# GpSimd writes 13 of the 16 last normed tiles, and the output products use four PSUM banks

## What is computed

```python
def _L1_ffn_ref(x, w_gate, w_up, w_down):
    def act_qdq(x):                       # one scale for the whole tensor
        scale = jnp.maximum(jnp.max(jnp.abs(x)) / 32767., 1e-12)
        return jnp.clip(jnp.round(x / scale), -32768., 32767.) * scale
    x = act_qdq(x)
    up = act_qdq(x @ lpbq_dequant(w_up).T)      # weights: 4 bits, blocks of 32
    gate = act_qdq(x @ lpbq_dequant(w_gate).T)
    sig = fixed_qdq_u16(jax.nn.sigmoid(gate))
    gate = act_qdq(gate * sig)
    o = act_qdq(gate * up)
    return o @ lpbq_dequant(w_down).T
...
x = x + tanh(g_xattn[1]) * _L1_xattn_ref(_layernorm(x), ctx_1024, ctx_1024, ...)
x = x + tanh(g_ffn[1]) * _L1_ffn_ref(_layernorm(x), ...)
```

## Time and profile before

| | |
|---|---|
| median of three runs | 1015.0 us |
| profiled execution | 1014.61 us |
| its span, first to last instruction | 1013.0 us |
| TensorE, VectorE, ScalarE, GpSimd busy | 883.8, 663.7, 477.7, 197.4 us |
| mean granted TensorE clock | 0.921 of 2.4 GHz |

### The profile page before, as it was taken

One profiled execution on the slowest core, in us unless ns is written; L12 is line 12 of the kernel. 1 busy time (PEld: TensorE's weight loads), 2 busy tenths in 40 slices (PEclk: granted clock), 3 DMA queues, 4 the chain that ended last, 5 costly groups with the idle time before them and its releaser, 6 DMA issues.

```text
span 1013.0 us, 13561 instructions
## 1 busy us (share of the span) xinstructions
PE 883.8 (87%) x4064; PEld 437.4 (43%) x4065; DVE 663.7 (66%) x1250; ACT 477.7 (47%) x612; POOL 197.4 (19%) x293
## 2 busy tenths in 40 slices
PE   3989999999974999999987699999999779990088
PEld 2542333333442666666654323333334444430077
DVE  5989888888350222222179788888886763598942
ACT  1323777777730111212132137777777363586650
POOL 3330101111136000000056212100006500124200
PEclk9886999999996999999997769999999999995589
DMA  7593856664243010111168763344310000000001
GB/s 226 151 279 56 206 127 168 162 174 147 88 142 134 32 31 31 31 36 36 49 214 232 176 144 75 85 86 85 80 38 2 1 1 0 1 0 0 0 32 52
DMA packets 71260, 91.45 MB, mean 90 GB/s; under 512 B 25894, under 2 KB 56870, under 8 KB 71206
## 3 DMA queue, kind: packets, MB, share of 16 engines
q1 hardware_dynamic: 62844, 67.38, 26.6%
q0 software_dynamic: 5584, 19.93, 5.9%
q10 hardware_dynamic: 2784, 3.54, 1.1%
HBM read 62.99 MB, written 27.44 MB: 89 GB/s over the span
## 4 chain that ended last, share of the span: by engine, by line
PE 75%; DVE 15%; DMA 4%; ACT 3%; issue 2%; SPq 0%; DVEq 0%; ACTq 0%
PE PS L1357 12%; PE PS L1389 12%; PE PS L1378 11%; PE PS L1518 8%; PE PS L1540 8%; PE PS L1616 6%; PE PS L1633 4%; PE PS L1332 4%; PE PS L1476 2%; DVE MX L1016 2%; PE PS L1529 2%; DMA X<-in_x 2%; PE PS L1340 1%; PE PS L1403 1%; DVE BIG L1254 1%
## 5 line engine op out<-in xcount | busy, mean ns | idle before, releaser
L1016 DVE TENSOR_REDUCE MX<-PS 128x1 f32<-128x512 f32 x512 | 320.1, 684 | 43.0 <-PE PS L1357 41.5
L749 ACT ACTIVATE Pt<-PS 128x1024 f32<-128x1024 f32 x256 | 248.6, 1022 | 113.0 <-PE PS L1378 113.0
L1357 PE MATMUL PS<-KSt,BIG 96*128 96x512 bf16 x512 | 188.0, 413 | 10.0 <-DVE PS L1039 5.3
L1378 PE MATMUL PS<-BIG,KSt 99*128 99x512 bf16 x512 | 153.2, 385 | 1.1 <-DMA BIG<-MR 1.1
L1389 PE MATMUL PS<-Pt,VS 128*17 128x512 f32 x1024 | 136.1, 598 | 0.0
L1357 PEld LDWEIGHTS PS<-KSt,BIG 96*128 96x128 bf16 x512 | 41.0, 99 | 163.6 <-DVE MX L1016 108.2
L1111 DVE COPY Pt<-PS 128x512 f32<-128x512 f32 x46 | 29.7, 687 | 88.1 <-PE PS L1529 88.1
L1616 PE MATMUL PS<-KSt,BIG 128*128 128x512 f32 x192 | 84.7, 602 | 2.2 <-DVE KSt L1208 2.2
L1518 PE MATMUL PS<-BIG,KSt 128*128 x184 | 85.5, 608 | 0.5 <-DVE KSt L1116 0.3
L1540 PE MATMUL PS<-BIG,Pt 128*128 x368 | 84.2, 382 | 1.2 <-DVE Pt L1111 1.0
L1378 PEld LDWEIGHTS PS<-BIG,KSt 99*128 99x128 bf16 x512 | 50.4, 99 | 56.0 <-issue 3.2
(11 more groups left out here) (160 smaller groups left out, 1045.9 us busy)
## 6 DMA issues: line engine op xcount, KB each, us to landing
qk_parts<-BIG SPq DMA_DIRECT2D x64, 192.0 KB
BIG<-in_w POOLq DMA_DIRECT2D x12, 1024.0 KB, 5.7
BIG<-qk_parts SPq DMA_DIRECT2D x32, 192.0 KB, 3.4
KSt<-qk_parts SPq DMA_DIRECT2D x32, 192.0 KB, 3.8
v_rows<-BIG SPq DMA_DIRECT2D x8, 544.0 KB
VS<-v_rows SPq DMA_DIRECT2D x32, 136.0 KB, 2.9
BIG<-qk_parts SPq DMA_DIRECT2D x32, 128.0 KB, 3.9
KSt<-qk_parts SPq DMA_DIRECT2D x32, 128.0 KB, 4.0
```

Of the source, the lines that this page charges most:

```text
L749: act.activation(PP[:, 2 * (kc % 2) + half, :, :].rearrange("p h t -> p (h t)"), ST[half], ACT.Exp, scale=DK ** -0.5).then_inc(exp_done, 1)
L1016: dve.tensor_reduce(MX[:, g % 2, i % TB, i // TB:i // TB + 1], ring(i), AX.X, ALU.max, negate=True).then_inc(max_taken, 1)
L1357: pe.matmul(ring(i), QS[0:ROWS, g, h, qc * P:(qc + 1) * P], KS[0:ROWS, g, h, :], start=True, stop=True).then_inc(max_done, 1)
L1378: last = pe.matmul(ST[half][:, i * S:(i + 1) * S], KS[0:ROWS + PARTS, g, h, kc * P:(kc + 1) * P], QS[0:ROWS + PARTS, g, h, :], start=True, ...
```

## The change

It does six things.

1. The norm parts become 6, 7 and 3 tiles. Variances, square roots and `rstd` are computed for the part's columns alone (`norm_cols`).
2. GpSimd writes the normed tiles of the first two parts, 13 tiles, when VectorE's `rstd` is there (`ln_rstd`), and counts them in `xf_pool`. These writes stand in GpSimd's order between the second and the third weight. VectorE writes the last 3 (`xf_own`).
3. VectorE makes the third weight's scales after the integer tiles instead of in the attention's last batch.
4. The tail's products use banks 2, 3, 4 and 5 in turn, in both layers.
5. TensorE takes the normed tiles of the first two batches, then weight 0, the third batch, weight 1, the fourth batch; ScalarE's copies follow this order, with the third square root behind two copies of weight 0 as before.
6. Weight 2 is transposed after 18 of the 24 gate banks instead of 12 (`W2_AT`).

The core of the diff (declarations of semaphores and blank lines left out):

```diff
@@ -372,6 +375,7 @@
         UP_DONE = -(-PIECES * 4 // 5)
+        W2_AT = BANKS * 3 // 4
         UP_EARLY = 6
@@ -380,7 +384,8 @@
         ORDER = [[0, 1, 2, 3], [2, 3, 0, 1]]
-        FFN_A, FFN_B, FFN_C = range(0, 6), range(6, 12), range(12, NT)
+        FFN_A, FFN_B, FFN_C = range(0, 6), range(6, 13), range(13, NT)
+        FFN_PARTS = {"ffn_a": FFN_A, "ffn_b": FFN_B, "ffn_c": FFN_C}
@@ -396,6 +401,13 @@
         NORM_BASE = {name: sum(len(t) for _, t in NORMS[:k]) for k, (name, _) in enumerate(NORMS)}
+        NORMS_BEFORE_FFN = NORM_BASE["ffn_a"]
+        def norm_cols(name):
+            part = FFN_PARTS.get(name, range(NT))
+            return slice(part[0], part[-1] + 1)
@@ -651,7 +663,7 @@
             gp.wait_ge(tg_bias, 2)
-            gp.wait_ge(xn_ready, NORM_BASE["ffn_a"])
+            gp.wait_ge(xn_ready, NORMS_BEFORE_FFN)
@@ -660,8 +672,19 @@
+            def write_norm(part, number):
+                gp.wait_ge(ln_rstd, number)
+                for i in part:
+                    t = x_tile(1, i)
+                    gp.tensor_scalar(XF[:, t, :], X[:, t, :], mv[:, i, 0:1], rstd[:, i:i + 1],
+                                     ALU.subtract, ALU.mult).then_inc(xf_pool, 1)
             steps = 0
             for k in range(3):
+                if k == 2:
+                    write_norm(FFN_A, 1)
+                    write_norm(FFN_B, 2)
                 gp.wait_ge(w_scales, k + 1)
@@ -697,7 +720,8 @@
                 act.wait_ge(ln_var, NORM_NO[name] + 1)
-                act.activation(sd[:, :], ve[:, :], ACT.Sqrt).then_inc(ln_sd, 1)
+                cols = norm_cols(name)
+                act.activation(sd[:, cols], ve[:, cols], ACT.Sqrt).then_inc(ln_sd, 1)
@@ -770,7 +794,7 @@
                     copy_turned(layer, i, i % 2)
-                    if layer and i == NT - 2:
+                    if layer and i == NT - 1:
                         norm("ffn_b")
@@ -823,14 +847,21 @@
-            copy_weight(0, (0, 1))
-            norm("ffn_c")
-            copy_weight(0, (2,))
-            for p in range(B):
+            def copy_nx(p):
                 b = ORDER[1][p]
...
                     act.activation(Q["xt"][:, c, b * S:(b + 1) * S], bank(p % 2 * 2 + c), ACT.Copy).then_inc(nxt_ready, 1)
+            copy_nx(0)
+            copy_nx(1)
+            copy_weight(0, range(2))
+            norm("ffn_c")
+            copy_weight(0, range(2, 3))
+            copy_nx(2)
+            copy_weight(1, range(3))
+            copy_nx(3)
@@ -846,11 +877,10 @@
-            copy_weight(1, range(3))
             act.activation(table[:, :], magic[:, 0:1], ACT.Sigmoid)
-            copy_banks(range(BANKS // 2))
+            copy_banks(range(W2_AT))
             copy_weight(2, range(3))
-            copy_banks(range(BANKS // 2, BANKS))
+            copy_banks(range(W2_AT, BANKS))
@@ -953,28 +983,36 @@
+            def late_stats(some):
+                for i in some:
+                    last = dve.bn_stats(stats[:, i, :], X[:, x_tile(1, i), :])
+                return last
             def norm(name, left=None):
...
                 norm_var(name)
-                norm_rstd(name)
+                link(dve, norm_rstd(name))
                 norm_write(NORM_TILES[name], XN)
...
-                for i in NORM_TILES[name]:
+                for i in FFN_PARTS.get(name, NORM_TILES[name]):
                     last = dve.bn_aggr(mv[:, i, :], stats[:, i, :])
                 link(dve, last)
-                dve.tensor_scalar(ve[:, :], mv[:, :, 1], EPS, None, ALU.add).then_inc(ln_var, 1)
+                cols = norm_cols(name)
+                dve.tensor_scalar(ve[:, cols], mv[:, cols, 1], EPS, None, ALU.add).then_inc(ln_var, 1)
...
+                cols = norm_cols(name)
                 dve.wait_ge(ln_sd, NORM_NO[name] + 1)
-                link(dve, dve.reciprocal(nw1[:, :], sd[:, :]))
-                link(dve, dve.tensor_tensor(nw2[:, :], ve[:, :], nw1[:, :], ALU.mult))
-                link(dve, dve.tensor_tensor(nw1[:, :], nw2[:, :], sd[:, :], ALU.add))
-                link(dve, dve.tensor_scalar(nw2[:, :], nw1[:, :], 0.5, None, ALU.mult))
-                link(dve, dve.reciprocal(rstd[:, :], nw2[:, :]))
+                link(dve, dve.reciprocal(nw1[:, cols], sd[:, cols]))
+                link(dve, dve.tensor_tensor(nw2[:, cols], ve[:, cols], nw1[:, cols], ALU.mult))
+                link(dve, dve.tensor_tensor(nw1[:, cols], nw2[:, cols], sd[:, cols], ALU.add))
+                link(dve, dve.tensor_scalar(nw2[:, cols], nw1[:, cols], 0.5, None, ALU.mult))
+                return dve.reciprocal(rstd[:, cols], nw2[:, cols])
@@ -1060,11 +1098,9 @@
                             update(layer, TB * (g - 2) + 2, 5)
-                            if layer and g == 2:
-                                weight_scales(2)
-                            elif layer:
+                            if layer and g == NG - 1:
                                 dve.wait_ge(x_upd, NT + FFN_A[-1] + 1)
-                                link(dve, norm_stats(x_tiles(FFN_A), "ffn_a"))
+                                link(dve, late_stats(FFN_A))
                                 norm_var("ffn_a")
@@ -1084,7 +1120,7 @@
                 for i in range(EARLY, NT):
-                    update(layer, i, 2 + i % 2)
+                    update(layer, i, 2 + i % 4)
@@ -1164,38 +1200,43 @@
-                update(1, i, 2 + i % 2)
-            norm_rstd("ffn_a")
+                update(1, i, 2 + i % 4)
+            norm_rstd("ffn_a").then_inc(ln_rstd, 1)
             update_late(8)
-            norm_write(x_tiles(FFN_A), XF)
+            dve.wait_ge(x_upd, NT + 9)
+            late_stats(range(6, 9))
             update_late(9)
-            dve.wait_ge(x_upd, NT + 9)
-            norm_stats(x_tiles(range(6, 9)), "ffn_b")
             update_late(10)
-            dve.wait_ge(xn_ready, NORM_BASE["ffn_b"])
+            dve.wait_ge(xf_pool, len(FFN_A))
             col_abs_max(0, 8, 6)
...
             dve.wait_ge(x_upd, NT + 12)
-            link(dve, norm_stats(x_tiles(range(9, 12)), "ffn_b"))
+            late_stats(range(9, 12))
+            update_late(12)
+            dve.wait_ge(x_upd, NT + 13)
+            link(dve, late_stats(range(12, 13)))
             norm_var("ffn_b")
-            update_late(12)
-            norm_rstd("ffn_b")
             update_late(13)
-            norm_write(x_tiles(FFN_B[0:2]), XF)
+            norm_rstd("ffn_b").then_inc(ln_rstd, 1)
             update_late(14)
-            norm_write(x_tiles(FFN_B[2:]), XF)
+            dve.wait_ge(x_upd, NT + 15)
+            late_stats(range(13, 15))
             update_late(15)
             dve.wait_ge(x_upd, 2 * NT)
-            link(dve, norm_stats(x_tiles(FFN_C), "ffn_c"))
+            link(dve, late_stats(range(15, NT)))
             norm_var("ffn_c")
-            dve.wait_ge(xn_ready, NORM_BASE["ffn_c"])
+            dve.wait_ge(xf_pool, len(FFN_A) + 2)
             col_abs_max(1, 14, 2)
-            norm_rstd("ffn_c")
-            norm_write(x_tiles(FFN_C), XF)
-            col_abs_max(2, 0, TB)
-            dve.wait_ge(xn_ready, NORM_BASE["ffn_c"] + len(FFN_C))
-            link(dve, col_abs_max(3, TB, TB))
+            link(dve, norm_rstd("ffn_c"))
+            for i in FFN_C:
+                t = x_tile(1, i)
+                dve.tensor_scalar(XF[:, t, :], X[:, t, :], mv[:, i, 0:1], rstd[:, i:i + 1],
+                                  ALU.subtract, ALU.mult).then_inc(xf_own, 1)
+            dve.wait_ge(xf_pool, len(FFN_A) + len(FFN_B))
+            col_abs_max(2, 0, 5)
+            dve.wait_ge(xf_own, len(FFN_C))
+            link(dve, col_abs_max(3, 5, 3))
             dve.tensor_reduce(cm[:, 0:1], cmx[:, 0:4], AX.X, ALU.max).then_inc(col_max, 1)
@@ -1207,6 +1248,7 @@
+            weight_scales(2)
@@ -1470,8 +1512,10 @@
                     pe.wait_ge(x_upd, t)
-                elif i >= EARLY + 2:
-                    pe.wait_ge(x_upd, t - 1)
+                elif i == EARLY + 3:
+                    pe.wait_ge(x_upd, NT * layer + EARLY)
+                elif i >= EARLY + 4:
+                    pe.wait_ge(x_upd, t - 3)
                 for c in range(KC):
@@ -1486,7 +1530,7 @@
                     if i > EARLY:
-                        project_out(layer, i - 1, 2 + (i - 1) % 2)
+                        project_out(layer, i - 1, 2 + (i - 1) % 4)
                     if i == EARLY:
@@ -1575,13 +1619,10 @@
-            turn_weight(0)
-            pe.wait_ge(on_evac, 2 * NT)
-            xf_ready = [NORM_BASE["ffn_a"] + TB, NORM_BASE["ffn_b"] + 2, NORM_BASE["ffn_c"], NORM_BASE["ffn_c"] + TB]
-            for p in range(B):
-                pe.wait_ge(xn_ready, xf_ready[p])
-                if p == 1:
-                    pe.wait_ge(x_upd, 2 * NT)
+            def turn_nx(p, pool, own):
+                pe.wait_ge(xf_pool, pool)
+                wait(pe, xf_own, own)
                 for c in range(KC):
@@ -1589,6 +1630,16 @@
+            pe.wait_ge(on_evac, 2 * NT)
```

(11 more changed lines are left out.)

3 lines of the change are left out of this document (added).

## The result

The changed kernel takes 1019.3 us (median of 12 runs, 1017.1 to 1023.9), the kernel before 1015.2 us (12 runs on the same chip): ratio 1.0038, 95% interval 1.0020 to 1.0057. The forecast was 1011.2 us and the range ended at 1013.4. The change makes the kernel slower, by 0.4%, not faster.

What follows compares the result with a forecast made beforehand. VectorE was taken to bound the stretch ending the second attention: 6.6 us removed from it, 2.9 lost to new waits, gain 3.7. 1014.6 - 3.7 = 1010.9, against the median 1011.3; given 1011.2 us, range 1009.0 to 1013.4.

Steps and rivals of the forecast that it cites:

- what GpSimd pays for a tile: GpSimd's write of one normed tile of 256 columns: 0.4 us, bounds 0.25 and 0.73.
- the walk: Second attention's tail, step by step to line 1199's operation: it starts at 817.15 instead of 820.87, gain 3.7 us.
- the pause ahead of product 15: TensorE's wait for update 14 before the last output product; not written down, its times leave about 1.6 us.
- The slower rival: Per-partition scalars make GpSimd's tile write dear; at 1.25 us a tile the kernel takes 1016.9 us; chance 0.04.
- The rival of the dearer GpSimd: GpSimd pays 0.73 us a tile, the first maximum waits 1.8 us: gain 1.9, 1012.7 us; chance 0.17.
- The clock: TensorE's clock stays full after the first pause, shortened to 1.77 us; low clock before the up/gate stage stays.
- the first rival: TensorE's clock falls at 797 all the same, later work comes 1.0 us later: gain 2.7, 1011.9 us; chance 0.22.
- more is gained in the up/gate stage: Rival: the up/gate stage starts at full clock, 1.7 us more gained, 1009.2 us; chance 0.08.
- the first round's multiply: VectorE's 16-column multiply at line 974 takes 0.17 us instead of 2.03, no longer waiting for GpSimd.
- product 15 is released by update 14: In the output products, tile 15 falls into bank 5 and waits for update 14, which ends at 807.7.
- the third root stands behind the weight copies: ScalarE's third square root follows two weight copies and ends at 812.55; VectorE loses 1.7 us.
- the third weight, moved behind the integer tiles: Its scales come at about 825 to 827.3, GpSimd is done at 837.6, TensorE asks at 852.7: 15 us slack.

Runs made afterwards that it cites:

- e_add: Changed kernel with GpSimd's tile writes as add of the negated mean, then multiply, instead of subtract, multiply; ratio 0.9971 to the kernel before.
- e_add_warm: e_add with 26 extra transposes that nobody reads, filling TensorE's pause ahead of product 15; ratio 0.9970 to the kernel before.
- e_scales: Kernel before with only the third weight's scales moved behind the integer tiles; ratio 0.9972 to the kernel before.
- e_bank5: Changed kernel with one condition mended, so products 11 and 15 no longer wait for all earlier updates; ratio 1.0015 to the kernel before.
- e_dve: Changed kernel with the mended bank-5 wait and VectorE writing all 16 normed tiles, GpSimd none; ratio 0.9965 to the kernel before.
- e_warm: Changed kernel with 56 extra transposes that nobody reads, ahead of TensorE's wait for update 14; ratio 1.0031 to the kernel before.
- e_add5w: Changed kernel with add, multiply writes, mended bank-5 wait, and 9 and 15 filler transposes around the maximum's spread; 1009.0 us, ratio 0.9923 to the kernel before.
- e_scalesw: Kernel before with the third weight's scales moved and 15 filler transposes behind the maximum's spread; ratio 0.9953 to the kernel before.

## Why the prediction was wrong

**The step that failed is "what GpSimd pays for a tile".** The forecast took 0.4 us, bounds 0.25 and 0.73; measured are 1.21. The straight line was drawn through operations that add and multiply, or take a minimum and a maximum, and no row showed a subtract followed by a multiply. The argument "the operation reads one tensor" took cost to depend on the operands; here it depends on the pair of operations. The Trainium skill, GPSIMD Engine Reference, section Engine selection, puts a one-input operation roughly at line rate. VectorE's 0.33 us against 0.54 for add, multiply is not far from that; 1.21 for subtract, multiply is. The prediction's 0.73 us "by that rule" doesn't follow from the page: 0.73 is a row with two tensors, and the write reads one.

**What it did to the walk**, from update 6 on, in us:

| moment | forecast | measured |
|---|---|---|
| first `rstd` written | 6.5 | 6.3 |
| update 10 ends | 9.1 | 8.6 |
| first maximum starts | 9.1 | 13.7 |
| second `rstd` written | 15.5 | 20.0 |
| product 15 ends | 17.1 | 22.6 |
| third root ends | 20.8 | 27.6 |
| line 1199's operation starts | 25.4 | 32.2 |

Up to update 10 the walk holds within 0.5 us. The dear write adds 4.6 us at the first maximum, about 6 x 0.8, and the rest of the difference to the end is 2.2 us.

**The second failed step is the pause ahead of product 15.** The prediction never writes it down; its times leave about 1.6 us for it, and full clock behind it. TensorE needed 1.09 us for each tile of the tail (797.88 to 798.97), not the 1.37 of the old order, so it came to the bank-5 wait earlier; and update 14, which releases it, came 4.4 us later. The pause was 7.42 us and the clock fell.

**How far the two go.** The difference of the stretch to the walk, 32.16 - 25.4 = 6.8 us, splits by single profiles: 3.66 from the changed kernel to e_add (write 1.21 to 0.54), 2.15 from there to e_add_warm (pause filled), and 0.95 from there to the walk. Of the last, the dearer write (0.54 and not 0.4, six times 0.14) and the first pause's clock would each account for most: in e_add_warm the sixth write and update 10 end 10.2 and 10.1 us after update 6, where the changed kernel's update 10 ended at 8.6. The run times bear out the first part alone: 1.0038 to 0.9971. The 2.15 us don't show in them, and e_add's profile is of the slowest of its twelve executions. So the price of the write is shown as the cause that turned a gain into a loss; how much of the loss the clock behind the pause makes in a typical execution stays open.

e_add_warm is the kernel that the forecast described, near enough; its stretch is 26.35 and its ratio 0.9970 (0.9959 to 0.9982), about the size forecast (1011.2 / 1015.0 = 0.9963). That is no proof of the walk: e_scales, without any tile write on GpSimd, has 0.9972.

**The slower rival was the right case**, with the right place and nearly the right sum: its formula gives line 1199 at 804.65 + 13 x 1.21 + 2.4 = 822.8 in the time of the kernel before, a stretch of 31.1, against 32.16. It left out the pause ahead of product 15 and its clock. Its chance of 0.04 was far too low, for the reason "no row shows so dear an operation": no row showed a cheap one of this kind either. And its cause, the scalars, is wrong (0.14 us of 1.21).

**The rival of the dearer GpSimd (0.73 a tile)** named its sign, the maximum waiting for a write. It also expected VectorE's small operations to meet writes: line 1014 took 0.37 us instead of 0.17 and ended with GpSimd's last write at 821.74. In e_bank5 the same line took 0.56. That is a small cost.

**The clock.** Forecast to stay at 1.00 behind the first pause, and it did in the changed kernel (products of 1.03 us after a pause of 1.75). That was no safe reading: in e_dve the first group after a pause of 1.75 took 1.02 us and not 0.65, in e_warm 1.09, in e_add_warm 1.12. There the first rival is the case (the clock falls at 797 all the same); it cost the first maximum 0.4 us between e_warm and the changed kernel, where the maximum waits for a write in any case, and not the 1.0 forecast. The rival "more is gained in the up/gate stage", chance 0.08, did not come in the changed kernel; e_scales (rest 188.3) and e_add5w (187.5) show that it exists.

**What went as forecast:** the first round's multiply is at 0.17 us; product 15 is released by update 14 through the bank-5 wait; the third root stands behind the weight copies and VectorE waits 2.73 us for it; the third weight, moved behind the integer tiles, makes nobody wait (the rest is 189.5 against 189.3).

**What stays open:** update 6 comes between 789.78 and 793.66 in these profiles, and nearly 3 us apart in kernels that are alike up to there. Its scatter is as large as most gains compared here, and no run tells what part of the measured 4.1 us comes from ahead of it in the median. Nor do the runs tell why the same pause sometimes costs the clock, or why the pair subtract, multiply is dear.

## What to carry to other kernels

Price an operation that moves to another engine by a row with the same pair of operations on that engine, or by a bench of a few instructions; equal shapes and input counts aren't enough, and the upper bound has to allow for this when no such row exists. Two causes in series can hide each other in a timeline (bank 5: 0.56 us of the stretch with dear writes, 3.81 with cheap ones), so try each also with the other one mended; and check the run times before you believe it, for here they showed no such difference. Try the parts of a change one by one: the smallest part, the move of the scales, has the ratio 0.9972 by itself. What the rest adds is not clearly shown even with the pauses filled: 0.9923 (0.9900 to 0.9946) in e_add5w against 0.9953 (0.9936 to 0.9970) in e_scalesw. After a stretch has been shortened, look at the granted clock of the next stage: part of the gain can be given back there.

## What the hardware showed

- On GpSimd, a 128x256 float32 write from one tensor with subtract, multiply takes 1.08 us with constants and 1.21 with two per-partition scalars; add, multiply 0.40 and 0.55; multiply, add with scalars 0.55.
- A lone subtract or add takes 0.85 us, more than the pair add, multiply.
- A subtract of two tensors takes 0.72 us and a multiply 0.61: cheaper than subtract, multiply on one.
- After pauses of 1.75 to 1.83 us TensorE's next group of four transposes took 0.65 us in some kernels and 1.02 to 1.12 us in others. Filling the pauses around the spread with transposes that nobody reads came with a full clock in the stage behind and a ratio of 0.9923 (0.9900 to 0.9946) instead of 0.9953 (0.9935 to 0.9971).
